# Attention output normalised in its transposed form, with row sums gathered by DMA

## The chip, the cores and the metric

The kernel runs on one core of a Trainium2 chip. Its time is the device time of one launch in microseconds (us), told as the median of three runs. One more launch was recorded by the hardware profiler; all rows below come from it.

## What is computed

One transformer block over x of 8 batches x 1024 tokens x 256: 16-head attention on the normalised input, and then a mixture-of-experts layer, each followed by a layer norm and a residual.

```
x = x + layernorm(attention(layernorm(x)))
x = x + layernorm(experts(layernorm(x)))

attention: q, k, v = split_heads(x @ w.T + b)         (16 heads of 16 columns)
           attn = softmax(q / sqrt(16) @ k.T)          (1024 x 1024 for each head)
           ctx  = attn @ v                             (joined to 256 columns)
           out  = ctx @ out_w.T + out_b
```

The change touches only the attention stage: how `ctx` is divided by the softmax's row sums and brought into the layout in which the output projection reads it.

## The kernel before

The program has two stages, one behind the other: attention (all 8 batches), then experts (16 groups of 512 tokens). Only the first is changed.

**Work of the attention stage.** A batch is cut into 8 steps of 8 units. Step s works on quad q = s // 2 (four heads) and on half f = s % 2 of the query tokens (512 of them); unit u = 8s + kc of the batch adds chunk kc of 128 keys. In a unit TensorE makes four score tiles (`st`, into `st_bank`), ScalarE takes their exponentials (`probs`), and TensorE multiplies them with the values (`pv`, into `o_bank`). For step s + 2 TensorE also makes four tiles of scores with the roles of queries and keys exchanged (`smax`, into three `sm_bank`s), and VectorE takes the maximum of each row (`reduce`, line 578). From these come the shifts of the exponentials: `combine_maxima` (line 585, two operands in SBUF), the job `SH` (a transposition), `shift_row`, and four small DMAs (`load_shift`) that put them into the stacked queries.

**Orders written by hand.** Each engine runs its own instruction list; semaphores join them. TensorE issues at most one job in a unit, by the table `JOBS`: (kind, batch offset, number, part). A job writes `job_bank`; ScalarE and VectorE read it one unit later. Jobs of half a projection are QK, V and OP (a unit each for its two parts), jobs of transpositions are XT, SH, OT and CT. `X_STATS`, `A_STATS` and `SEEDS` put VectorE's layer-norm work into units.

**The attention output before.** `o_bank` holds for each of the four heads 32 rows: 16 of output, one of the row sum (a column of ones behind the values, `VW = DH + 1`), the rest unused. At the first unit of the next step ScalarE copies it to `o_sb` (`store_o`, line 501). Job OT (8 per batch, units 10, 18, ... and unit 2 of the next batch) transposes it with four 128 x 128 passes, VectorE takes the reciprocals of the sums (line 623, 128 x 16) and multiplies (line 627) into `ctx_tok`, tokens on partitions. Job CT (4 per batch, units 0, 3, 11 and 12 of the next batch) transposes `ctx_tok` back, and ScalarE and VectorE split it in a high and a low part (`cT`, lines 478 and 605). Job OP (the output projection, units 5 to 8, 15, 16, 20, 21) reads `cT`.

**Pool** (GpSimd) normalises x for the next batch, adds the output bias (line 738), does the Newton steps of the reciprocal roots (lines 719 to 725), the normalisation of the attention output (751), the residual (755) and the copies of the values (744). **SP** issues every DMA, in one list: 14 for each quad's stack of queries and keys (`load_stack`, lines 220 and 224), 4 for each `load_shift` (line 233), and the loads and stores of x.

Units and steps are told here by their number in the batch; unit 64 is unit 0 of the next one. Waits on a counter stand in the instruction list, so what is queued behind a waiting instruction on its engine waits too.

## Time and profile before

| | us |
|---|---|
| median of three runs | 2961.0 (2960.58 to 2962.13) |
| profiled execution, its own time | 2961.11 |
| span of the profiled execution | 2959.3 |
| attention stage, up to its last store | 0 to about 1707 |
| one batch in the middle of it (492.72 to 689.99) | 197.27 |
| expert stage | from about 1710 |

Busy shares of the whole span are 95% for TensorE, 76% for VectorE, 56% for ScalarE and 18% for Pool; TensorE's granted clock is at its full level (2.4 GHz) in nearly all slices, and falls at the start and between the stages. These shares mix two stages with different limits, so the attention stage is read by batches and units. A timeline row gives start, duration, engine, line, operation and operands; rows of equal instructions that follow each other are merged, with their number behind x.

### The profile page before, as it was taken

The numbers are of one execution on the slowest core, as the hardware profiler recorded it, in microseconds if no ns is written. First come the engines' busy times: TensorE is split into PE (matmuls) and PEld (weight loads), VectorE is DVE, ScalarE is ACT, GpSimd is POOL, SyncE is SP. The second block draws the span as 40 slices with busy tenths as digits, with TensorE's granted clock in tenths as the row PEclk, the third lists the DMA queues.
The fourth block names the chain that finished last, engine by engine and source line by source line (L and its number), as shares of the span: only waits on it lengthen the run. The fifth ranks groups of instructions, "written<-read, shape, count | busy, mean of one in ns | idle before, by whom it ended". The sixth has DMA issues, their size and how long they took to land. (4 is left out here: it accounts for less than half of the span.)

```text
span 2959.3 us, 47558 instructions
## 1 busy us (share of the span) xinstructions
PE 2805.3 (95%) x16898; PEld 1718.8 (58%) x16898; DVE 2259.0 (76%) x4788; ACT 1643.3 (56%) x3095; POOL 541.0 (18%) x664
## 2 busy tenths in 40 slices
PE   5999999999999999999999659999999999999997
PEld 3434443443444434434443348888888888888886
DVE  5898999999989999999898146666666666666654
ACT  1577777777777777777777424333333333333332
POOL 4010220310312203103112220111111111111112
PEclk8899999999999999999999769999999999999999
DMA  5203332233133322330330033222322222232221
GB/s 91 44 17 50 44 73 38 51 51 52 31 58 45 73 37 51 52 51 17 57 44 23 22 110 108 79 79 79 78 78 79 80 79 79 78 78 79 79 72 54
DMA packets 120396, 180.59 MB, mean 61 GB/s; under 512 B 14160, under 2 KB 76768, under 8 KB 118112
## 3 DMA queue, kind: packets, MB, share of 16 engines
q1 hardware_dynamic: 120160, 177.55, 27.6%
q8 instruction: 135, 2.21, 0.3%
q14 instruction: 101, 0.83, 0.1%
HBM read 108.81 MB, written 17.30 MB: 43 GB/s over the span
## 5 line engine op out<-in xcount | busy, mean ns | idle before, releaser
L578 DVE TENSOR_REDUCE score_max<-sm_bank 128x1 f32<-128x512 f32 x2048 | 1305.2, 681 | 115.8 <-PE sm_bank L314 107.9
L511 ACT ACTIVATE probs<-st_bank 128x512 f32<-128x512 f32 x2048 | 1097.8, 598 | 346.8 <-PE st_bank L302 345.0
L314 PE MATMUL sm_bank<-qk_stack 64*128 64x512 f32 x2048 | 793.2, 462 | 21.6 <-DMA qk_stack<-qk_stack 10.6
L302 PE MATMUL st_bank<-qk_stack 64*128 64x512 f32 x2048 | 748.0, 449 | 21.7 <-ACT probs L511 20.8
L314 PEld LDWEIGHTS sm_bank<-qk_stack 64*128 64x128 f32 x2048 | 327.2, 187 | 574.8 <-DVE score_max L578 529.3
L324 PE MATMUL o_bank<-probs,v_quad 128*32 128x512 f32 x4096 | 545.4, 605 | 8.5 <-ACT o_sb L501 7.3
L1263 DVE TENSOR_TENSOR gated<-gate_act,u_bank 128x512 f32<-128x512 f32 x256 | 175.8, 687 | 311.1 <-ACT gate_act L1094 311.1
L1094 ACT ACTIVATE gate_act<-g_bank 128x512 f32<-128x512 f32 x272 | 162.5, 598 | 429.0 <-PE u_bank L1000 428.8
L302 PEld LDWEIGHTS st_bank<-qk_stack 64*128 64x128 f32 x2048 | 307.9, 184 | 72.3 <-ACT probs L511 49.3
L1105 ACT ACTIVATE h_hi<-h 128x512 fp32r<-128x512 f32 x272 | 172.0, 632 | 317.8 <-DVE h L1266 283.3
L1014 PE MATMUL y_bank<-f_w_hi,h_hi 128*128 128x256 f32 x1088 | 311.8, 287 | 5.9 <-DVE h_lo L1274 5.8
L1014 PE MATMUL y_bank<-f_w_hi,h_lo 128*128 128x256 f32 x1088 | 305.1, 280 | 0.0
L1014 PE MATMUL y_bank<-f_w_lo,h_hi 128*128 128x256 f32 x1088 | 303.7, 279 | 0.0
L1364 POOL TENSOR_SCALAR f_x_in<-f_x_in,f_mv,f_rstd 128x256 f32<-128x256 f32 x64 | 90.8, 1431 | 707.3 <-DVE f_rstd L1175 707.3
L1274 DVE TENSOR_TENSOR h_lo<-h,h_hi 128x512 fp32r<-128x512 f32 x272 | 185.5, 682 | 44.9 <-ACT h_hi L1105 41.6
L1000 PE MATMUL g_bank<-f_xT_lo,f_w_hi 128*128 128x512 f32 x544 | 216.7, 398 | 0.0
L1000 PE MATMUL g_bank<-f_xT_hi,f_w_hi 128*128 128x512 f32 x544 | 215.2, 396 | 1.5 <-DVE gated L1263 1.5
L1000 PE MATMUL g_bank<-f_xT_hi,f_w_lo 128*128 128x512 f32 x544 | 216.1, 397 | 0.0
L1000 PE MATMUL u_bank<-f_xT_hi,f_w_hi 128*128 128x512 f32 x544 | 215.8, 397 | 0.0
L1000 PE MATMUL u_bank<-f_xT_lo,f_w_hi 128*128 128x512 f32 x544 | 215.6, 396 | 0.0
L1000 PE MATMUL u_bank<-f_xT_hi,f_w_lo 128*128 128x512 f32 x544 | 215.4, 396 | 0.0
L1014 PEld LDWEIGHTS y_bank<-f_w_hi,h_hi 128*128 128x128 f32 x1088 | 205.3, 189 | 16.7 <-DVE h_lo L1274 6.5
(186 smaller groups left out, 3490.7 us busy)
## 6 DMA issues: line engine op xcount, KB each, us to landing
cb<-comb_dram SPq DMA_DIRECT2D x256, 256.0 KB, 3.7
qk_stack<-qk_parts SPq DMA_DIRECT2D x384, 128.0 KB
x_in<-in_x SPq DMA_DIRECT2D x8, 1024.0 KB, 6.4
x_res<-in_x SPq DMA_DIRECT2D x16, 512.0 KB, 3.8
x<-x_res SPq DMA_DIRECT2D x16, 512.0 KB, 2.9
f_x_in<-x SPq DMA_DIRECT2D x16, 512.0 KB, 3.9
f_x_res<-x SPq DMA_DIRECT2D x16, 512.0 KB, 7.1
out<-f_x_res SPq DMA_DIRECT2D x16, 512.0 KB, 3.2
```

Source lines behind the costliest of these rows:

```text
L302: mm(st_bank[tile % RING][:, :], k_stack[q][p][rows, kc * CH:(kc + 1) * CH], q_stack[q][p][rows, f * HALF:(f + 1) * HALF], start=True, sto ...
L314: mm(sm_bank[n % RING][:, :], q_stack[q][p][rows, tok:tok + CH], k_stack[q][p][rows, half * HALF:(half + 1) * HALF], start=True, stop=True ...
L324: last = mm(o_bank[32 * j:32 * j + 32, :], v_quad[q][:, kc, VW * j:VW * j + 32], probs[0 if kc % 2 == 0 else 1][:, j, :], start=(kc == 0), ...
L511: nc.scalar.activation(probs[kc % 2][:, j, :], st_bank[(4 * U + j) % RING][:, :], ACT.Exp).then_inc(exp_done, 1)
L578: v.reduce_max(score_max[f][:, HC * (2 * p + e) + c, half:half + 1], sm_bank[n % RING][:, :], AX_X).then_inc(smax_read, 1)
L1000: last = mm(bank[:, :], w[b][:, e, col + k * HID:col + (k + 1) * HID], xT[par][a][:, k, :], start=(t == 0), stop=(t == len(steps) - 1))
L1014: last = mm(y_bank[:, c, :], h[i][a][:, c * CH:(c + 1) * CH], w[b][:, e, 2 * D:3 * D], start=(e == 0 and t == 0 and c % 2 == 0), stop=(e = ...
L1094: a_(gate_act[i][:, :], g_bank[i][:, :], ACT.Silu).then_inc(S["silu_done"], 1)
L1105: a_(h[i][0][:, :], h32[i][:, :], ACT.Copy).then_inc(S["h_hi_done"], 1)
L1263: v.tensor_tensor(gated[:, :], gate_act[i][:, :], u_bank[i][:, :], ALU.mult).then_inc(S["gated_done"], 1)
L1274: v.tensor_tensor(h[i][1][:, :], h32[i][:, :], h[i][0][:, :].bitcast(F32), ALU.subtract).then_inc(S["h_ready"], 1)
L1364: gp.tensor_scalar(x_in[:, c, :], x_in[:, c, :], mv[:, c, 0:1], rstd[:, c:c + 1], ALU.subtract, ALU.mult).then_inc(S["f_x_normed"], 1)
```

## The change

- `VW` becomes 32: behind the 16 columns of values stand 16 columns of ones, so each head has 16 rows of output and 16 equal rows of sums in `o_bank`. The matmul's shape (128 x 32 weights) stays. The ones are set once, by Pool, in `v_quad`; the setting of `v_stage` by VectorE goes.
- The jobs OT and CT go, with VectorE's small reciprocals and multiplications, and `ctx_tok`. `store_o` stays.
- `gather` (SP, 8 DMAs of 32 KB per step, 64 per batch): the 16 output rows of each head go to `o_part[f]`, its sum rows to `sum_part[f]`, at the partitions in which the projection wants them. Two quads fill one such tile of 128 x 512.
- Four times a batch (f, k): VectorE writes a first guess of the reciprocal from the bits of the sums (`sum_recip`, one 128 x 512 operation, units 27, 35, 59 and 4 of the next batch), Pool does three Newton steps and the multiplication (`divide`, ten 128 x 512 tensor_tensor), and ScalarE and VectorE split the result (`split_hi`, `split_lo`, units 39, 46, 3, 11), now from SBUF. The very last one uses VectorE's reciprocal in place of guess and steps.
- `cT` becomes one pair for each half. `qk_parts` is halved in size, the first batch's second half of it lies in `probs`; the first exponential therefore waits for stacks 2 and 3 of batch 0, and stack 3 is loaded ahead of the first `load_shift(0, 1)`.

```diff
+SPLITS = {39: (0, 0, 0), 46: (0, 1, 0), 3: (-1, 0, 1), 11: (-1, 1, 1)}
+RECIPS = {27: (0, 0, 0), 35: (0, 1, 0), 59: (0, 0, 1), 4: (-1, 1, 1)}
 JOBS = {
-    0: ("CT", -1, 0, None), 3: ("CT", -1, 1, None), 11: ("CT", -1, 2, None), 12: ("CT", -1, 3, None),
-    2: ("OT", -1, 7, None),
...
-    if _s:
-        JOBS[8 * _s + 2] = ("OT", 0, _s - 1, None)
...
+            def gather(B, s):
+                q, f = s // 2, s % 2
+                if q % 2 == 0 and B + q > 0:
+                    sp.wait_ge(ctx_split, split_no(B, f, 0) + 1 if q else split_no(B - 1, f, 1) + 1)
+                sp.wait_ge(o_stored, STEPS * B + s + 1)
+                for j in range(4):
+                    to = 64 * (q % 2) + DH * j
+                    sp.dma_start(o_part[f][to:to + DH, :], o_sb[32 * j:32 * j + DH, :]).then_inc(gathered, 16)
+                    sp.dma_start(sum_part[f][to:to + DH, :], o_sb[32 * j + DH:32 * j + 2 * DH, :]).then_inc(gathered, 16)
...
             def batch(b, first, last, next_last):
                 if not first:
+                    gather(b - 1, 7)
                     load_residual(b - 1, 0)
                 load_shift(b, 1)
-                if first:
-                    sp.wait_ge(stacks_set, 5 * QUADS)
-                else:
+                if not first:
                     load_stack(b, 2, False)
-                load_stack(b, 3, first)
-                load_shift(b, 2)
-                load_shift(b, 3)
-                load_shift(b, 4)
+                    load_stack(b, 3, False)
+                for s in range(3):
+                    gather(b, s)
+                    load_shift(b, s + 2)
...
+                gather(b, 3)
                 load_shift(b, 5)
                 if not last:
                     load_stack(b + 1, 0, False)
+                gather(b, 4)
                 load_shift(b, 6)
                 if not first:
                     store_x1(b - 1, 1)
                 if not last:
                     load_stack(b + 1, 1, False)
+                gather(b, 5)
                 load_shift(b, 7)
+                gather(b, 6)
                 if not last:
                     load_shift(b, 8)
...
+            def split_hi(B, f, k):
+                act.wait_ge(divided, split_no(B, f, k) + 1)
...
+                nc.scalar.activation(cT[f][0][:, k, :], o_part[f][:, :], ACT.Identity,
+                                     bias=bias[:, 2, k:k + 1]).then_inc(ctx_hi, 1)
...
+                        if j == 0 and U == 0:
+                            act.wait_ge(stack_loaded[2], STACK_INC)
+                            act.wait_ge(stack_loaded[3], STACK_INC)
...
+            def sum_recip(B, f, k):
+                dve.wait_ge(gathered, GATHER_INC * (STEPS * B + 4 * k + 2 + f + 1))
+                n = split_no(B, f, k)
+                if n:
+                    dve.wait_ge(divided, n)
+                if n + 1 < split_no(BATCHES, 0, 0):
+                    v.tensor_scalar(recip[:, :].bitcast(I32), sum_part[f][:, :].bitcast(I32), -1, RECIP_SEED,
+                                    ALU.mult, ALU.add).then_inc(recip_begun, 1)
+                else:
+                    v.reciprocal(recip[:, :], sum_part[f][:, :]).then_inc(recip_begun, 1)
+            def split_lo(B, f, k):
+                dve.wait_ge(ctx_hi, split_no(B, f, k) + 1)
+                v.scalar_tensor_tensor(cT[f][1][:, k, :], o_part[f][:, :], bias[:, 2, k:k + 1],
+                                       cT[f][0][:, k, :].bitcast(F32), ALU.add, ALU.subtract).then_inc(ctx_split, 1)
...
+            def divide(B, f, k):
+                n = split_no(B, f, k)
+                wait_apart(pool, recip_begun, n + 1, passed["pool"])
+                if n + 1 < split_no(BATCHES, 0, 0):
+                    for i in range(3):
+                        if i:
+                            pool.wait_ge(recip_chain, 9 * n + 3 * i)
+                        g.tensor_tensor(recip_tmp[:, :], sum_part[f][:, :], recip[:, :], ALU.mult).then_inc(recip_chain, 1)
+                        pool.wait_ge(recip_chain, 9 * n + 3 * i + 1)
+                        g.tensor_tensor(recip_tmp[:, :], two[:, :].to_broadcast([128, HALF]), recip_tmp[:, :],
+                                        ALU.subtract).then_inc(recip_chain, 1)
+                        pool.wait_ge(recip_chain, 9 * n + 3 * i + 2)
+                        g.tensor_tensor(recip[:, :], recip[:, :], recip_tmp[:, :], ALU.mult).then_inc(recip_chain, 1)
+                    wait_apart(pool, recip_chain, 9 * (n + 1), passed["pool"])
+                g.tensor_tensor(o_part[f][:, :], o_part[f][:, :], recip[:, :], ALU.mult).then_inc(divided, 1)
...
             def batch(b, first, last):
                 copy_v(b, 3, first)
                 if not first:
+                    divide(b - 1, 1, 1)
                     add_bias(b - 1, 0)
                 if not last:
                     norm_x(b + 1)
                 if not first:
                     residual(b - 1, 0)
                     add_bias(b - 1, 1)
+                divide(b, 0, 0)
+                divide(b, 1, 0)
+                if not first:
                     residual(b - 1, 1)
                 if not last:
                     for q in range(3):
                         copy_v(b + 1, q, False)
+                divide(b, 0, 1)
```

Where the two lists of an engine stand apart, three places show it. VectorE, before, in units 1 to 4 of batch 1 (`cT_lo` is the second half of a CT job, `recip` and `ctx_tok` an OT job, the reductions are the row maxima):

```order
L605 SCALAR_TENSOR_TENSOR cT_lo<-job_bank,bias,cT_hi 128x512
L578 TENSOR_REDUCE score_max<-sm_bank 128x1 x4
L616 TENSOR_SCALAR shift_row<-job_bank 16x128
...
L623 RECIPROCAL recip<-job_bank 128x16
L627 TENSOR_TENSOR ctx_tok<-job_bank,recip 128x4x64
L578 TENSOR_REDUCE score_max<-sm_bank 128x1 x4
L605 SCALAR_TENSOR_TENSOR cT_lo<-job_bank,bias,cT_hi 128x512
```

VectorE, changed, units 3 to 4 and the first of unit 8 of a batch:

```order
L660 SCALAR_TENSOR_TENSOR cT_lo<-o_part,bias,cT_hi 128x512
...
L653 TENSOR_SCALAR recip<-sum_part 128x512
...
L618 TENSOR_TENSOR row_max<-score_max 128x16
L611 TENSOR_REDUCE score_max<-sm_bank 128x1 x2
L571 BN_STATS stats<-x_in 128x6
```

The reads of `job_bank` are gone; one operation on `o_part` and one on `sum_part` take their place, both with all operands in SBUF. SP, before, from the end of stack 3 (`load_stack(b, 3)`) on:

```order
L220 DMA qk_stack<-qk_parts 16x2048
L220 DMA qk_stack<-qk_parts 16x2x1024
L224 DMA qk_stack<-qk_stack 1x2x1024 x2
L233 DMA qk_stack<-shift_row 1x4x128 x12
L242 DMA x<-x_res 128x4x256
```

SP, changed, the same place:

```order
L248 DMA qk_stack<-qk_stack 1x2x1024 x2
L268 DMA o_part<-o_sb 16x512
L269 DMA sum_part<-o_sb 16x512
L268 DMA o_part<-o_sb 16x512
L269 DMA sum_part<-o_sb 16x512
L268 DMA o_part<-o_sb 16x512
L269 DMA sum_part<-o_sb 16x512
L268 DMA o_part<-o_sb 16x512
L269 DMA sum_part<-o_sb 16x512
L257 DMA qk_stack<-shift_row 1x4x128 x4
```

Eight DMAs of `gather` now stand between the stack and the shifts of step 2. Pool, changed, behind the bias of the second half: of what ran there before (the residual's Newton steps on 128 x 4) a `divide` of ten such rows now stands ahead, and another:

```order
L777 TENSOR_TENSOR attn_out<-attn_out,out_bias 128x512 x2
L786 TENSOR_TENSOR recip_tmp<-sum_part,recip 128x512
L788 TENSOR_TENSOR recip_tmp<-two,recip_tmp 128x512
L791 TENSOR_TENSOR recip<-recip,recip_tmp 128x512
...
L793 TENSOR_TENSOR o_part<-o_part,recip 128x512
```

## Rows read from the trace of the kernel before

**Rows 1.** Windows: length; busy PE, PEld, DVE, ACT, POOL; clock; DMA share; GB/s.

```profile
492.72:689.99 197.27, 193.87 (x1242) 79.94 (x1240) 184.32 (x346) 153.39 (x290) 38.77 (x62) 1.00 0.29 50
```

**Rows 2.** Timeline of TensorE, units 16 to 19 of that batch.

```profile
542.79 1.07 PE L324 MATMUL o_bank<-probs,v_quad 128*32 128x512 f32 x8
546.02 1.07 PE L324 MATMUL o_bank<-probs,v_quad 128*32 128x512 f32 x8
548.72 1.06 PE L324 MATMUL o_bank<-probs,v_quad 128*32 128x512 f32 x8
551.68 1.06 PE L324 MATMUL o_bank<-probs,v_quad 128*32 128x512 f32 x8
```

**Rows 3.** Timeline of VectorE, units 3 and 4 of that batch.

```profile
503.18 0.17 DVE L542 BATCH_NORM_AGGREGATE mv_x<-stats 128x2 f32<-128x6 f32 x1
503.27 0.22 DVE L623 RECIPROCAL recip<-job_bank 128x16 f32<-128x16 f32 x1
503.53 0.42 DVE L627 TENSOR_TENSOR ctx_tok<-job_bank,recip 128x256 f32<-128x256 f32 x1
503.87 2.47 DVE L578 TENSOR_REDUCE score_max<-sm_bank 128x1 f32<-128x512 f32 x4
506.26 0.74 DVE L605 SCALAR_TENSOR_TENSOR cT_lo<-job_bank,bias,cT_hi 128x512 fp32r<-128x512 f32 x1
506.92 0.68 DVE L578 TENSOR_REDUCE score_max<-sm_bank 128x1 f32<-128x512 f32 x1
```

**Rows 4.** Timeline of VectorE: statistics of x between two pairs of row maxima.

```profile
514.04 0.42 DVE L538 BATCH_NORM_STATS2 stats<-x_in 128x6 f32<-128x256 f32 x1
514.38 1.32 DVE L578 TENSOR_REDUCE score_max<-sm_bank 128x1 f32<-128x512 f32 x2
```

**Rows 5.** Durations by line (minimum/median/maximum in ns): a VectorE operation on 128 x 512 in SBUF.

```profile
L638 DVE TENSOR_SCALAR x_res<-probs x1: 427/427/427, 11.0 to 11.0; 128x512 f32<-128x512 f32 x1
```

**Rows 6.** Groups of instructions of the batch: Pool on 128 x 512 in SBUF.

```profile
L738 POOL TENSOR_TENSOR attn_out<-attn_out,out_bias 128x512 f32<-128x512 f32 x4 | 5.1, 1278 | 28.4 <-ACT attn_out L484 28.4
```

**Rows 7.** Timeline of the stage's end: ScalarE, Pool and SP.

```profile
1661.67 0.60 ACT L501 ACTIVATE o_sb<-o_bank 128x512 f32<-128x512 f32 x1 [1.18 <-PE o_bank L324]
1680.37 0.20 POOL L719 TENSOR_TENSOR newton_a<-rstd_a 128x4 f32<-128x4 f32 x1 [2.02 <-DVE rstd_a L560]
1680.64 0.20 POOL L721 TENSOR_TENSOR newton_a<-newton_a,var_a 128x4 f32<-128x4 f32 x1
1691.19 2.48 POOL L738 TENSOR_TENSOR attn_out<-attn_out,out_bias 128x512 f32<-128x512 f32 x2
1706.63 0.37 SPq L242 DMA_DIRECT2D x<-x_res  x1
```

**Rows 8.** Timeline of SP's DMA issues, units 2 to 27 of the batch.

```profile
500.45 2.43 SPq L233 DMA_DIRECT2D qk_stack<-shift_row  x4
...
516.29 11.10 SPq L220 DMA_DIRECT2D qk_stack<-qk_parts  x12
527.44 1.32 SPq L224 DMA_DIRECT2D qk_stack<-qk_stack  x2
528.80 47.54 SPq L233 DMA_DIRECT2D qk_stack<-shift_row  x12
```

**Rows 9.** Timeline of ScalarE and SP ahead of the first unit.

```profile
77.65 35.67 SPq L233 DMA_DIRECT2D qk_stack<-shift_row  x8
102.32 3.10 ACT L511 ACTIVATE probs<-st_bank 128x512 f32<-128x512 f32 x6
```

**Rows 10.** Timeline, VectorE beside Pool: once in the expert stage, once in attention.

```profile
2913.76 2.40 POOL L1375 TENSOR_TENSOR f_x_res<-y,f_x_res 128x1024 f32<-128x1024 f32 x1 [0.18 <-POOL y L1371]
2914.60 2.10 DVE L1266 TENSOR_TENSOR h<-gated,cb 128x512 f32<-128x512 f32 x1
...
564.41 4.83 POOL L751 TENSOR_SCALAR attn_out<-attn_out,mv_a,rstd_a 128x256 f32<-128x256 f32 x4 [0.22 <-POOL rstd_a L725]
...
567.47 0.17 DVE L585 TENSOR_TENSOR row_max<-score_max 128x16 f32<-128x16 f32 x1
```

More of the change, by code:

```diff
@@ L17 @@
 RING = 3
-VW = DH + 1
+VW = 2 * DH
 EXPERTS, HID, TOPK = 16, 128, 8
@@ L441, in _ @@
                 batch(b, b == 0, b == BATCHES - 1)
-            job("OT", BATCHES - 1, 7)
-            for i in range(2):
-                job("CT", BATCHES - 1, i)
-            for i in range(2):
-                job("OP", BATCHES - 1, i)
-            for i in range(2, 4):
-                job("CT", BATCHES - 1, i)
-            for i in range(2, 4):
+            for i in range(4):
                 job("OP", BATCHES - 1, i)
@@ L516, in batch @@
                         kind, off, i, part = JOBS[u - 1]
-                        if kind in ("XT", "QK", "V", "CT", "OP") and part != 0:
+                        if kind in ("XT", "QK", "V", "OP") and part != 0:
                             job(kind, b + off, i)
+                    if u in SPLITS and not (first and SPLITS[u][0]):
+                        off, f, k = SPLITS[u]
+                        split_hi(b + off, f, k)
             for b in range(BATCHES):
@@ L522, in _ @@
             store_o(STEPS * BATCHES)
-            for f in range(2):
-                for kind in ("CT", "OP"):
-                    for i in (2 * f, 2 * f + 1):
-                        job(kind, BATCHES - 1, i)
+            split_hi(BATCHES - 1, 0, 1)
+            job("OP", BATCHES - 1, 0)
+            job("OP", BATCHES - 1, 1)
+            split_hi(BATCHES - 1, 1, 1)
+            job("OP", BATCHES - 1, 2)
+            job("OP", BATCHES - 1, 3)
         @block.vector
@@ L673, in batch @@
                         reduce(S + 2, (s + 2) % STEPS, kc, 0)
+                    if u in SPLITS and not (first and SPLITS[u][0]):
+                        off, f, k = SPLITS[u]
+                        split_lo(b + off, f, k)
+                    if u in RECIPS and not (first and RECIPS[u][0]):
+                        off, f, k = RECIPS[u]
+                        sum_recip(b + off, f, k)
                     if not last and u in X_STATS:
@@ L692, in _ @@
                 batch(b, b == 0, b == BATCHES - 1)
-            job("OT", BATCHES - 1, 7)
+            split_lo(BATCHES - 1, 0, 1)
+            sum_recip(BATCHES - 1, 1, 1)
             for f in range(2):
-                job("CT", BATCHES - 1, 2 * f)
-                job("CT", BATCHES - 1, 2 * f + 1)
+                if f == 1:
+                    split_lo(BATCHES - 1, 1, 1)
                 for c in range(HC):
@@ L757, in _ @@
             pool.sem_inc(x1_ready, 1)
+            g.memset(two[:, :], 2.0).then_inc(two_set, 1)
+            wait_apart(pool, two_set, 1, passed["pool"])
             set_stacks(0)
```

116 lines of the change are left out of this document (54 added, 62 removed).

## The prediction

> **What bounds the kernel now.** I read the table of windows first: in one batch of 197.27 us TensorE is busy for 193.87 and VectorE for 184.32, ScalarE has a fifth to spare and Pool is idle for 158 [rows 1]. Two engines are almost full, so the next view is the timeline of TensorE, unit by unit, from one group of `pv` matmuls to the next. Unit 16 carries half a projection and takes 546.02 - 542.79 = 3.23; unit 17 carries only SH, 2.70; unit 18 carries OT, 2.96 [rows 2]. All 64 spacings of the batch, read in this way, fall into these kinds: 32 units with half a projection at 3.19 to 3.23, where TensorE sets the pace; light ones at 2.70 to 2.75; single transposition jobs at 2.90 to 2.96; and some at 3.04 to 3.49, which are in units 1 to 4 and 11 to 13.
>
> Those last ones are VectorE's. Four row maxima back to back take 506.26 - 503.87 = 2.39, and up to 2.47 with the start of the next; I use 2.47 a unit. An OT job costs it 503.87 - 503.27 = 0.60, a CT job 506.92 - 506.26 = 0.66 [rows 3]. Statistics of x cost 514.38 - 514.04 = 0.34 [rows 4], their aggregation 503.27 - 503.18 = 0.09 [rows 3], so 0.44 together. So units with a CT or OT read and statistics come to 3.0 to 3.13, above a light unit's 2.70, and the three score banks let VectorE lag by about a microsecond before TensorE waits. In units with half a projection VectorE has 0.75 to spare.
>
> **What goes.** Batches 1 to 6, by groups of units, spacing now against the larger of 2.70 (2.91 with XT) and VectorE's new sum:
> - Units 0 to 4 take 15.30 now. New: 5 x 2.47, two statistics 0.88, SH and `row_max` 0.30, one split 0.66, one guess 0.4: 14.6. Saved 0.7.
> - Units 9 to 14 take 17.98. New: 6 x 2.47, three statistics 1.32, SH 0.2, one split 0.66: 17.0. Saved 1.0.
> - Units 18 and 19 take 6.05, new 5.4. Saved 0.6.
> - Units 26 and 27: 0.2; 33 and 34: 0.35; 42, 50 and 58, each 2.91 to 2.70: 0.6.
> The sum is 3.45, say 3.4 a batch. In units with half a projection nothing is saved, and the 48 transposition passes are worth less than their TensorE time, since part of it filled waits.
>
> The guess (`sum_recip`) is not in the trace in its form. A tensor_scalar on 128 x 512 in SBUF took 0.43 [rows 5], the split on as many elements 0.74 [rows 3]; I take 0.4 of pitch, near the first, because it is the same kind of operation. At the upper end the four cost 0.3 more each, of which units 27, 35 and 59 hide theirs and unit 4 doesn't: 0.3 a batch.
>
> **What comes, beside other work.** A `divide` is ten tensor_tensor on 128 x 512 in a chain. Pool does one in 1.28 [rows 6]; from one Newton step to the next the pitch is 0.27 for an operation of 0.20 [rows 7], a gap of 0.07. So 10 x 1.28 + 9 x 0.07 = 13.4, with the start about 13.7, 4.4 units. Pool's 39 us a batch become 39 + 4 x 13.4 = 92 of 194. Each result is due later: the guess of unit 27 ends in unit 32 and is split in 39; 35 in 40, for 46; 59 in 0, for 3; 4 in 9, for 11. The tightest, the last, has nearly two units left, and the bias and residual work behind it waits for no more than it did. Pool's length is hidden.
>
> The gathers are 8 issues a step. Four small issues take 2.43, 0.6 each; a stack's larger ones 11.10 / 12 = 0.93 [rows 8]. I take 0.6, the row with the small transfer, so 4.8 a step; SP's list has the room. The place to look at is behind stacks 2 and 3. Now their last issue ends at about 528.8 and the shifts of step 2 go straight behind [rows 8]. With `gather(b, 0)` ahead they are issued by 528.8 + 4.8 + 2.4 = 536.0. TensorE wants them for the first score tile of step 2, about 0.66 ahead of the `pv` of unit 15, which started 3.23 before 542.79 [rows 2]: at 538.9, and some 1.0 sooner in the changed kernel, 537.9. That leaves 1.9 for landing: taken as nothing, 1.9 a batch if the gathers issue at 0.93. The shifts of step 6 stand the same way behind `gather(b, 4)`, with half a microsecond less at stake.
>
> Batch 0: the first exponential waits for stack 3. The shift ahead of it starts at 77.65, takes 2.4, then 14 issues of 0.93 end at 93.1; the first exponential is at 102.32 [rows 9]. Hidden by 9 us. Were that cover gone it would cost up to the 13 us of the stack.
>
> **What comes, in the way.** VectorE's `row_max` and `split_lo` read two tensors in SBUF, and so does Pool's tensor_tensor. In the expert stage one such VectorE operation was started 0.84 into a Pool tensor_tensor and took 2.10 in place of 0.69, ending 0.54 behind Pool's end: it stood still for 1.41. Beside a Pool tensor_scalar `row_max` took its usual 0.17 [rows 10]. Now Pool hardly does a tensor_tensor in attention while VectorE reads two SBUF tensors. In the changed kernel `row_max` of unit 8 and `split_lo` of unit 39 fall inside a `divide`; `row_max` of units 32, 40 and 64 fall at or just behind the end of one. A stop lasts as long as what is left of one Pool operation, 0 to 1.28, 0.64 on average. At unit 64 VectorE sets the pace: I charge 0.4 (it may miss). At unit 8 a fifth is absorbed: 0.5. At 32 the slack of half-projection units takes it: 0. At 39 two splits, the QK one and the new one, meet a stop, 2.47 + 1.32 + 0.64 = 4.4 against 3.22, and unit 40 adds `row_max`: a lag of 1.5 of which a microsecond is bearable; 0.6. Together 1.5 a batch (0 to 6.4, all five whole and none absorbed).
>
> The Trainium skill, "SBUF — State Buffer", section "Who interferes with whom", says that a VectorE instruction with two SBUF inputs and a GpSimd instruction that reads SBUF lock each other out for the whole instruction, the later one waiting. The first pair of rows agrees, with 1.41; the second does not, since `row_max` ran through beside a tensor_scalar.
>
> **The stage's end.** From the last `store_o` at 1661.67 to the last store at 1706.63 it is 45.0 [rows 7]. Now half 0 goes first, on the chain OT, CT, CT, OP, OP, bias, statistics, and Pool's Newton steps start at 1680.37; half 1's bias waits for Pool until 1691.19. New: the divide of (7, 0, 1) begins in unit 60, about 1651, and ends at 1664.6; split 1.5, two OP jobs of 3.5 each: 1673.2. The gather of step 7 lands at about 1661.7 + 0.7 + 4.8 + 2 = 1669.2; the reciprocal takes 0.43 at least [rows 5], and I take 0.7, then Pool's multiplication, 1671.2; bias, statistics and seed of half 0 end at about 1676.8, which is 3.5 before 1680.37, and what follows on Pool keeps its length. 3 saved. The reciprocal's far end is 7.0 (0.22 for 16 columns [rows 3], scaled by 32), which would turn this into a loss of 3.
>
> **The sum.** Batches 1 to 6: 6 x (3.4 - 1.5) = 11.4. Batch 0 has no OT 7 and no CT: by its own spacings 2.0, less 0.5. Batch 7 has no row maxima in its last steps, where an OT unit is as long as a light one (2.68): 2.9, less 0.5. End 3. Together 18.3: the profiled execution goes from 2961.11 to 2943, and so does the median, which lies 0.1 from it. The expert stage is unchanged.
>
> **The rivals.**
> - *Pool's stops don't reach TensorE.* For: a stop is short, `row_max` is tiny. Against: units 0 to 4 leave no slack. 6 x 3.4 + 4.9 + 3 = 28: 2933. Chance 0.25.
> - *The shifts come late.* `gather` moves the shifts of steps 2 and 6 behind 16 more issues. For: 1.9 us of room. Against: the 0.6 of the small issues. 1.9 + 0.8 a batch, seven batches, 19: 2962, within 0.2% of before. Chance 0.12.
> - *Slower: the shared access to SBUF.* One mechanism, at units 8, 32, 39, 40 and 64 while Pool divides: all stops near 1.28, and not absorbed, since behind units 8, 32 and 40 VectorE-bound units follow. Six batches x (6.4 - 3.4) = 18, batches 0 and 7 about even, end -3: 2976 at most, 2968 in the middle. It decides from 3.4 a batch, which is 0.68 a stop with nothing absorbed. By the rule of the Trainium skill's page named above this is the case, since each of the five is a lock-out. Chance 0.18.
> - The forecast itself, 2943: 0.45.
>
> **How the numbers follow.** A difference within 0.2% (5.9 us) can't be told from none. The forecast and the first rival are faster: 0.70. The late shifts are mostly the same: 0.13 with a rest of the others. Slower: 0.17. The range goes down to 2931, below the first rival by the error of its sum, and up to 2964, over the late shifts and to the nearer part of the slower case; beyond it I leave somewhat under 0.2.
>
> **What would show it.** Units 18, 42, 50 and 58 at 2.70; batches of 195.4 in place of 197.27 (193.9 without stops, 200 with whole ones); durations of `row_max` above 0.17 and of `split_lo` above 0.74 in units 8 and 39; no wait of `st` for a DMA of the shifts; Pool near 92 us a batch; the last store 42 behind the last `store_o`. The prediction is wrong if `sum_recip` waits for a gather (VectorE idle before it), if Pool's operations on 128 x 512 are longer than 1.28 so that a split waits, or if the DMA issues are.

## The result, and the profile after

The changed kernel takes 2942.4 us (median of four runs, 2941.2 to 2944.3) against 2961.1 for the kernel before, run beside it on the same chip: a ratio of 0.9937, with an interval of 0.9920 to 0.9954. The profiled execution spans 2942.6 us where that of before spans 2959.3, so 16.7 less; it was the slowest of the four (2944.3). The last store of the attention stage is issued at 1690.62, before at 1706.63 [rows 7].

First the page of the changed kernel: busy time of each engine, and its DMA issues with size and time to landing. Pool went from 18% to 31%.

```profile
PE 2772.4 (94%) x16514; PEld 1689.3 (57%) x16514; DVE 2241.8 (76%) x4691; ACT 1635.6 (56%) x3095; POOL 916.9 (31%) x976
...
o_part<-o_sb SPq DMA_DIRECT2D x256, 32.0 KB, 1.9
sum_part<-o_sb SPq DMA_DIRECT2D x256, 32.0 KB, 2.0
```

The same batch as in [rows 1], in windows (length; busy PE, PEld, DVE, ACT, POOL; clock; DMA share; GB/s), of the changed kernel:

```profile
488.96:683.43 194.47, 189.98 (x1194) 76.61 (x1192) 181.90 (x334) 152.36 (x290) 86.87 (x103) 1.00 0.34 61
```

TensorE has 3.9 us less to do and the batch is 2.8 shorter, with 48 matmuls fewer; Pool has 48 us more, and no engine waits for a result of Pool's. The units of [rows 2], 16 to 19, in the changed kernel:

```profile
537.35 1.06 PE L364 MATMUL o_bank<-probs,v_quad 128*32 128x512 f32 x8
540.57 1.06 PE L364 MATMUL o_bank<-probs,v_quad 128*32 128x512 f32 x8
543.27 1.07 PE L364 MATMUL o_bank<-probs,v_quad 128*32 128x512 f32 x8
546.24 1.06 PE L364 MATMUL o_bank<-probs,v_quad 128*32 128x512 f32 x8
548.95 1.06 PE L364 MATMUL o_bank<-probs,v_quad 128*32 128x512 f32 x8
```

Read as there: unit 16 3.22, unit 17 2.70, unit 18 2.97, unit 19 2.71. Unit 18 kept its 2.97 though its transposition job is gone, and unit 19 fell to a light unit from 3.09 (6.05 for the two before, less the 2.96 of [rows 2]). In unit 18 TensorE waits for VectorE to read a score bank, here as a timeline row of TensorE in that unit:

```profile
545.21 0.50 PE L354 MATMUL sm_bank<-qk_stack 64*128 64x512 f32 x1 [0.21 <-DVE score_max L611]
```

VectorE has statistics of the attention output and the shifts to make there besides its row maxima, so it is VectorE that holds this unit at 2.97.

Between batches there is now a spread that the kernel before did not have. From step 0 to step 0, batches 1 to 6 take 194.90, 194.47, 197.76, 194.18, 195.36 and 194.19; before, each took 197.2 to 197.3. The reason stands in the table of waits of the changed kernel, window 300 to 1500 (engine, tile and line, what was waited for: us in total, times, longest):

```profile
PEld st_bank L342 <- DMA qk_stack<-shift_row: 7.0, 6, 2.6
PE st_bank L342 <- DMA qk_stack<-shift_row: 4.6, 4, 2.2
```

TensorE waits for the shifts. The longest of these is in the batch of 197.76. Timeline of SP and TensorE there, around units 13 to 15 (start, duration, engine, line, operation, operands, number; in brackets the wait ahead of it and its releaser):

```profile
717.20 1.85 SPq L248 DMA_DIRECT2D qk_stack<-qk_stack  x2
719.15 0.58 SPq L268 DMA_DIRECT2D o_part<-o_sb  x1
...
721.04 1.62 SPq L269 DMA_DIRECT2D sum_part<-o_sb  x1
...
724.85 0.58 SPq L269 DMA_DIRECT2D sum_part<-o_sb  x1
725.48 2.53 SPq L257 DMA_DIRECT2D qk_stack<-shift_row  x4
...
729.69 0.57 PE L342 MATMUL st_bank<-qk_stack 64*128 64x512 f32 x2 [2.19 <-DMA qk_stack<-shift_row]
...
730.35 1.85 PE L364 MATMUL o_bank<-probs,v_quad 128*32 128x512 f32 x8
```

The eight issues of `gather` stand between the stack and the shifts, one of them at 1.62 in place of 0.59. The shifts are issued by 728.01 and TensorE goes on at 729.69. Its `pv` group behind the wait then takes 1.85 in place of 1.06, and the windows say why (same columns as above):

```profile
724.00:728.00 4.00, 3.25 (x21) 1.22 (x21) 3.58 (x7) 2.95 (x6) 0.00 (x0) 1.00 0.14 34
728.00:732.00 4.00, 2.31 (x11) 0.45 (x11) 2.07 (x5) 1.28 (x3) 0.00 (x0) 0.81 0.01 3
732.00:736.00 4.00, 4.00 (x26) 2.01 (x22) 2.62 (x7) 2.54 (x5) 0.00 (x0) 0.76 0.02 5
736.00:740.00 4.00, 4.00 (x30) 1.82 (x26) 3.52 (x9) 2.87 (x7) 1.41 (x7) 1.00 0.21 52
```

The granted clock falls from 1.00 to 0.81 and 0.76, so part of these windows ran at the lower of its two levels (1.2 in place of 2.4 GHz): (0.19 + 0.24) x 4.00 = 1.7 us of full clock are missing, which is 3.4 us at half. It is back from 736 on. Units 14 and 15 took 4.80 and 4.78 where 2.74 and 3.24 are usual.

The second thing to look at are VectorE's two-operand reads beside Pool. Timeline of both at unit 8, and at unit 39, of the batch from 488.96:

```profile
513.82 1.28 POOL L791 TENSOR_TENSOR recip<-recip,recip_tmp 128x512 f32<-128x512 f32 x1
513.91 1.23 DVE L618 TENSOR_TENSOR row_max<-score_max 128x16 f32<-128x16 f32 x1
...
608.76 1.28 POOL L793 TENSOR_TENSOR o_part<-o_part,recip 128x512 f32<-128x512 f32 x1 [0.18 <-POOL recip L791]
609.65 0.94 DVE L660 SCALAR_TENSOR_TENSOR cT_lo<-o_part,bias,cT_hi 128x512 fp32r<-128x512 f32 x1
```

`row_max`, 0.17 alone, is started 0.09 into Pool's operation and ends 0.04 behind it. `split_lo`, 0.74 alone, takes 0.94. The durations of `row_max` between 300 and 1500 (minimum/median/maximum in ns) show that most of the 49 miss Pool; the long ones are those of unit 8, one in each batch:

```profile
L618 DVE TENSOR_TENSOR row_max<-score_max x49: 174/176/1253, 319.0 to 1489.7; 128x16 f32<-128x16 f32 x49
```

Third, the end of the stage, to be read against [rows 7]. Timeline of the last `pv`, the last `store_o`, the last reciprocal, Pool and SP:

```profile
1645.44 1.94 PE L364 MATMUL o_bank<-probs,v_quad 128*32 128x512 f32 x8 [1.16 <-ACT probs L539]
1647.44 0.60 ACT L519 ACTIVATE o_sb<-o_bank 128x512 f32<-128x512 f32 x1 [2.05 <-PE o_bank L364]
1654.63 3.35 DVE L656 RECIPROCAL recip<-sum_part 128x512 f32<-128x512 f32 x1 [5.20 <-DMA sum_part<-o_sb]
1658.16 1.26 POOL L793 TENSOR_TENSOR o_part<-o_part,recip 128x512 f32<-128x512 f32 x1 [11.07 <-DVE recip L656]
1659.38 2.48 POOL L777 TENSOR_TENSOR attn_out<-attn_out,out_bias 128x512 f32<-128x512 f32 x2
...
1690.62 0.37 SPq L277 DMA_DIRECT2D x<-x_res  x1
```

From the last `store_o` to the last store it is 43.18, before 44.96. The bias of half 0 stands behind Pool's multiplication, and that waits for a reciprocal of 3.35.

### The profile page after: what moved, and what is told of

It reads as the page before. It is cut to its first block and busy times, and to the rows that moved or that the text cites. A ratio compares the mean times of both kernels' runs of the same rounds, so it can differ in the third digit from the quotient of the medians.

```text
span 2942.6 us, 47567 instructions
## 1 busy us (share of the span) xinstructions
PE 2772.4 (94%) x16514; PEld 1689.3 (57%) x16514; DVE 2241.8 (76%) x4691; ACT 1635.6 (56%) x3095; POOL 916.9 (31%) x976
## 5 line engine op out<-in xcount | busy, mean ns | idle before, releaser
L354 PE MATMUL sm_bank<-qk_stack 64*128 64x512 f32 x2048 | 804.1, 465 | 18.6 <-DMA qk_stack<-qk_stack 10.9
L342 PE MATMUL st_bank<-qk_stack 64*128 64x512 f32 x2048 | 761.6, 453 | 37.9 <-ACT probs L539 31.3
L342 PEld LDWEIGHTS st_bank<-qk_stack 64*128 64x128 f32 x2048 | 316.7, 184 | 119.3 <-ACT probs L539 91.7
L786 POOL TENSOR_TENSOR recip_tmp<-sum_part,recip 128x512 f32<-128x512 f32 x93 | 119.2, 1282 | 488.4 <-DVE recip L653 483.5
```

What stands on the lines that cost most here:

```text
L342: mm(st_bank[tile % RING][:, :], k_stack[q][p][rows, kc * CH:(kc + 1) * CH], q_stack[q][p][rows, f * HALF:(f + 1) * HALF], start=True, sto ...
L354: mm(sm_bank[n % RING][:, :], q_stack[q][p][rows, tok:tok + CH], k_stack[q][p][rows, half * HALF:(half + 1) * HALF], start=True, stop=True ...
L786: g.tensor_tensor(recip_tmp[:, :], sum_part[f][:, :], recip[:, :], ALU.mult).then_inc(recip_chain, 1)
```

## The experiments

Each is measured beside the kernel before, on the same chip, but the groups ran on different chips, on which the kernel before took 2959.4 to 2961.1. So differences of about 1 us between groups mean little. The attention stage's end (issue of the last store of x) is given beside the time, because the expert stage, the same in all kernels, took 1251.5 to 1254.8 in the profiled executions compared here, a spread that small differences drown in.

**The two suspects of the prediction, one at a time.** The first kernel takes the `gather`s out of the shifts' way at four places:

```diff
                 for s in range(3):
-                    gather(b, s)
                     load_shift(b, s + 2)
+                    gather(b, s)
...
-                gather(b, 4)
                 load_shift(b, 6)
+                gather(b, 4)
```

> The changed kernel with load_shift ahead of gather for steps 2, 3, 4 and 6; nothing else moves. Theory (gathers push the shifts of step 2 past the moment at which TensorE wants them, and TensorE's clock falls in the gap): the waits of st for the shift DMAs, 11.6 us between 300 and 1500 in the changed kernel's trace, vanish, batches all take 194.2, unit 14 is 2.7 in each; 5 to 8 us less than the changed kernel, 2935 to 2938. Rival (TensorE's waits there only stand in for VectorE's, which would end as late): within 1.5 us of the changed kernel.

Measured: 2994.1 us, ratio 1.0117 (1.0103 to 1.0130); the stage ends at 1738.27. No theory had this. Unit 14 is at 2.73 in every batch, so the late shifts are gone; but a new wait has come, in each batch at the guess of unit 27. Timeline of SP and VectorE of this kernel:

```profile
781.41 2.51 SPq L257 DMA_DIRECT2D qk_stack<-shift_row  x4
783.96 0.56 SPq L268 DMA_DIRECT2D o_part<-o_sb  x1
...
788.35 0.59 SPq L269 DMA_DIRECT2D sum_part<-o_sb  x1
...
790.32 0.43 DVE L653 TENSOR_SCALAR recip<-sum_part 128x512 int32<-128x512 int32 x1 [4.91 <-DMA sum_part<-o_sb]
```

`gather(b, 2)` now stands behind `load_shift(b, 4)`, whose own data, the shifts of step 4, are made only in units 24 to 26. So the rows of step 2, ready since unit 24, leave SP at 783.96 to 788.94, and VectorE stands before `sum_recip` for 4.91 with all its row maxima queued behind it. TensorE's row behind it, and the windows from there on (columns as before):

```profile
791.40 0.79 PE L354 MATMUL sm_bank<-qk_stack 64*128 64x512 f32 x1 [4.24 <-DVE score_max L611]
...
790.90:797.72 6.82, 6.32 (x24) 2.49 (x24) 5.43 (x10) 2.95 (x6) 6.41 (x6) 0.50 0.58 167
```

TensorE stands still for 4.24, and then its granted clock is at the lower level for 6.8. Units 28 and 29 take 8.82 and 4.50 in place of 3.12 and 3.22: 7.0 more, of which 4.2 are the wait and the rest falls in the stretch at the lower level. The same edit with the next one added (below) gave 2993.3, ratio 1.0112: the same wait, where the two gains had been expected to add.

The expectation above counts TensorE's waits for the shifts as 11.6. That adds PEld's 7.0 and PE's 4.6, which are the same landings seen twice; by the lengths of units 14 and 15 it is 5.7 in batches 1 to 6.

> The shifts ahead of the gathers, and the one-input row_max together. Theory: the two gains add, 7 to 11 us less than the changed kernel, 2932 to 2936, and 25 to 29 less than the kernel before. Rival (they hide behind the same units): no more than the larger of the two alone.

**Take away what meets Pool.** `row_max` as a reduction, which has one operand in SBUF:

```diff
-                v.tensor_tensor(row_max[:, :], score_max[f][:, :, 0], score_max[f][:, :, 1],
-                                ALU.max).then_inc(row_max_ready, 1)
+                v.reduce_max(row_max[:, :], score_max[f][:, :, :], AX_X).then_inc(row_max_ready, 1)
```

> The changed kernel with row_max made by one tensor_reduce over the two halves' columns in place of a tensor_tensor, so that it reads one SBUF tensor. Theory (a VectorE operation with two SBUF inputs stops behind a Pool tensor_tensor): row_max never takes above 0.3, unit 8 goes from 3.50 to 3.22, 2 to 3.5 us less than the changed kernel. Rival (the stop is of the access to SBUF as such, or the long row_max is absorbed): unit 8 stays at 3.50, within 0.8 us of the changed kernel.

Measured: 2943.0 (2938.9 to 2949.5), ratio 0.9945 (0.9933 to 0.9958). Timeline beside Pool at unit 8 of this kernel:

```profile
511.32 1.29 POOL L790 TENSOR_TENSOR recip<-recip,recip_tmp 128x512 f32<-128x512 f32 x1
511.39 0.19 DVE L618 TENSOR_REDUCE row_max<-score_max 128x16 f32<-128x32 f32 x1
```

Its durations between 300 and 1500 (minimum/median/maximum in ns):

```profile
L618 DVE TENSOR_REDUCE row_max<-score_max x49: 185/186/188, 317.5 to 1483.3; 128x16 f32<-128x32 f32 x49
```

The reduction runs through inside Pool's operation, in all 49 cases. Unit 8 goes from 3.50 to 3.22 and unit 9 from 2.78 to 2.71 in batches 1 to 6. The mechanism is shown, and its price with it: 0.35 a batch. The time as a whole didn't fall by the 2 to 3.5 that were expected. In its profiled execution the late shifts take 4.1 in units 14 and 15 (one unit 14 of 4.33), against 2.1 in the second profile of the changed kernel (below), which is most of what the reduction gains; and its times spread over 10 us.

The next kernel leaves out Pool's three Newton steps (the output is divided with the rough guess), so that Pool hardly works:

```diff
-                if n + 1 < split_no(BATCHES, 0, 0):
+                if False:
                     for i in range(3):
```

> The changed kernel with the nine Newton operations of each divide left out (the first guess is multiplied as it is, so the division is rough); Pool does one 128x512 tensor_tensor in place of ten. Theory (Pool's 13 us a divide are hidden, and cost only the stops of row_max and split_lo): like the kernel with the one-input row_max and 0.2 a batch more, 3 to 5 us less than the changed kernel. Rival (Pool's length matters, since later work on Pool ends later): 8 us or more less.

Measured: 2942.1 (2939.6 to 2945.4), ratio 0.9940 (0.9927 to 0.9952). Units 8 and 9 are at 3.22 and 2.71 again, unit 40 at 3.21 in place of 3.26; unit 39 stays at 3.33, so that is not Pool's doing: two splits fall in it on ScalarE too. 36 of Pool's operations a batch removed give 0.35 in units 8 and 9 and 0.05 in unit 40, and nothing in the other units of batches 1 to 6, those of the late shifts aside. Pool's length is hidden. The time missed its 3 to 5 as well: its late shifts take 7.5 in its profiled execution.

**The late shifts, without the new wait.** Only the two `gather`s whose place matters are moved; `gather(b, 2)` stays ahead of `load_shift(b, 4)`. The changed kernel was run again beside it:

```diff
-                for s in range(3):
+                load_shift(b, 2)
+                gather(b, 0)
+                for s in range(1, 3):
                     gather(b, s)
                     load_shift(b, s + 2)
...
-                gather(b, 4)
                 load_shift(b, 6)
+                gather(b, 4)
```

> The changed kernel as it is, for the comparison on one chip. Both theories expect 15 to 20 us less than the kernel before. Theory (the shift DMAs of step 2 land late by another amount in each execution): its unit 14s differ from batch to batch, 2.7 to 5, and its times spread by 3 to 8 us, where the kernel before spreads by 2 to 4.

> The changed kernel with only the shifts of steps 2 and 6 issued ahead of the gathers of steps 0 and 4, whose results VectorE wants much later; the other gathers stay where they are. Theory (late shifts cost the changed kernel 4 to 8 us, and the 50 us of the first reordering came from a late gather that VectorE waited for): 4 to 8 us less than the changed kernel, no wait for shift DMAs, unit 14 at 2.7 in all batches, no wait of the guess in units 27. Rival (any gather behind a shift delays something of its own): no less, or more than the changed kernel.

Measured: the changed kernel again 2943.0 (2942.3 to 2948.1); with the two moved 2937.5 (2936.6 to 2940.3), ratio 0.9926 (0.9914 to 0.9939), the stage's end at 1684.16. Timeline of SP in this kernel at the place shown above (its step began 1.0 sooner):

```profile
715.76 2.31 SPq L248 DMA_DIRECT2D qk_stack<-qk_stack  x2
718.11 2.49 SPq L257 DMA_DIRECT2D qk_stack<-shift_row  x4
720.70 0.58 SPq L268 DMA_DIRECT2D o_part<-o_sb  x1
```

The shifts leave SP straight behind the stack and no wait for them is left in the table of waits. So the late shifts cost 5.5 us of the changed kernel's time by the medians. By single executions it varies, as the wait does: the stage ends 6.5 sooner than in the first profile of the changed kernel, 2.6 sooner than in the second (1686.77), and units 14 and 15 hold 5.9 of it in the first and 2.1 in the second, whose unit 14s lie between 2.73 and 3.88.

**Both mended.** The two moved `gather`s and the reduction together:

> Those two shifts first and row_max with one SBUF input. Theory: unit 8 at 3.22 instead of 3.50 in seven batches and the last batch's unit 40 at 2.7 instead of 3.3: 2.5 us less than with the shifts alone, 22 to 28 less than the kernel before, with a spread below 3 us. Rival (the stops are absorbed): the same as with the shifts alone.

Measured: 2936.0 (2934.7 to 2936.5), ratio 0.9918 (0.9905 to 0.9932), the stage's end at 1680.39. In time 1.5 less than with the `gather`s alone, in the stage's end 3.8 less, of which 0.9 was there when step 1 of batch 0 began; unit 32 of batch 7 went from 3.26 to 2.71 and unit 8 of every batch but the first to 3.22. The expectation had named unit 40 of batch 7 for this; that stays at 3.66, since `split_lo` still meets Pool there. Its batch, in windows:

```profile
487.11:681.01 193.90, 189.45 (x1194) 76.35 (x1192) 181.03 (x334) 152.23 (x290) 86.84 (x103) 1.00 0.35 61
```

All six middle batches lie between 193.7 and 193.9.

**Where the 3.4 a batch are.** On this base, what the change took away is given back, to each engine apart and to both, without its waits for other engines: four 128 x 128 transpositions per step that nobody reads; and on VectorE one reduction over 128 x 512 per step (0.66, where an OT job cost 0.60).

```diff
+    JOBS[8 * _s + 2] = ("TR", 0, _s, None)
...
+                if kind == "TR":
+                    for c in range(HC):
+                        nc.tensor.transpose(job_bank[:, c * CH:(c + 1) * CH], ident[:, :], ident[:, :])
```

```diff
+                    if kc == 3:
+                        v.reduce_max(spare[:, S:S + 1], two_wide[:, :], AX_X)
```

> The kernel with the two shifts first and the one-input row_max, and with four 128x128 transpositions of a constant put back on TensorE in units 2, 10, ..., 58 of each batch (the places of the OT jobs; nobody reads them). Theory (a single transposition job costs a light unit 0.2): units 18, 26, 34, 42, 50 and 58 from 2.70 to 2.91, units 2 and 10 less since VectorE sets their pace: 8 to 12 us more than without them. Rival (the gain came from VectorE alone): under 3 us more.

> The same base with one VectorE operation of about 0.6 (a tensor_reduce on 128x512 in SBUF, no wait, nobody reads it) put back in units 3, 11, ..., 59, the places of the OT reads. Theory (VectorE has no slack in units 0 to 4 and 9 to 14 only): units 3, 11 and 19 longer, 1.2 to 2 us a batch, 8 to 15 us more in all. Rival (TensorE's jobs alone set the time): under 3 us more.

> Both put back. Theory (in a unit the longer of TensorE's and VectorE's work counts, and the lag of a microsecond joins neighbouring units): more than either, less than the sum, 15 to 22 us more than the base, which leaves only the CT jobs and the end of the stage as gain over the kernel before. Rival (they are independent): the exact sum.

Measured: TensorE's share back 2946.1, ratio 0.9947 (0.9934 to 0.9959); VectorE's 2951.3, 0.9965 (0.9951 to 0.9979); both 2957.2, 0.9988 (0.9980 to 0.9997). So 10.2, 15.3 and 21.2 more than the base, where the parts add up to 25.5; each is 0.7 less if measured from the kernel before, which took 0.7 more on this chip. The same batch in the three, in this order, one line of each kernel's windows:

```profile
489.75:684.84 195.09, 191.90 (x1226) 78.70 (x1224) 181.40 (x334) 152.88 (x290) 86.88 (x103) 1.00 0.34 61
```

```profile
491.36:687.26 195.90, 190.17 (x1194) 76.56 (x1192) 185.40 (x342) 152.54 (x290) 87.04 (x102) 1.00 0.34 61
```

```profile
492.50:689.20 196.70, 192.69 (x1226) 78.91 (x1224) 185.59 (x342) 153.12 (x290) 87.06 (x103) 1.00 0.34 61
```

TensorE is given 2.5 us more work and the batch grows by 1.2; VectorE 4.4 and it grows by 2.0. Unit by unit: the transpositions cost 0.21 each in units 2, 26, 34, 42, 50 and 58, of which unit 3 gives 0.08 back, and nothing in 10 and 18, which stay at 2.97 with or without them (the expectation had 18 growing). VectorE's reduction costs 0.60 in units 3 and 11 (2.78 to 3.38) and 0.28 in 19; the one of unit 27 costs 0.07 there and 0.2 in 28; those of 35, 43, 51 and 59 cost nothing in their own units.

Unit 40 grows too, by 0.28, and that is not VectorE's load. The reduction of unit 35 stands ahead of the guess, so Pool divides later and `split_lo` of unit 39 meets Pool's last multiplication at another point. Timeline of Pool and VectorE in the kernel with VectorE's share back:

```profile
612.55 1.29 POOL L798 TENSOR_TENSOR o_part<-o_part,recip 128x512 f32<-128x512 f32 x1 [0.18 <-POOL recip L796]
613.14 1.24 DVE L663 SCALAR_TENSOR_TENSOR cT_lo<-o_part,bias,cT_hi 128x512 fp32r<-128x512 f32 x1
```

It takes 1.24 here in every batch, 0.94 in the base and with TensorE's share back, and 1.09 with both. It was TensorE and VectorE both, in different units: 1.2 a batch for TensorE, 1.7 for VectorE, 0.3 for Pool's stop, which the test itself brought in.

**The stage's end.** Two kernels on the base of the two mended places. In one, the very last division uses the guess without Newton steps in place of VectorE's reciprocal, so that its result is rough:

```diff
-                if n + 1 < split_no(BATCHES, 0, 0):
+                if True:
                     v.tensor_scalar(recip[:, :].bitcast(I32), ...
```

> The same again, with VectorE's last reciprocal on 128x512 (3.35 us in the changed kernel's trace) replaced by the tensor_scalar guess (0.42), without Newton steps, so the last division is rough. Theory (this reciprocal lies on the chain that ends the stage): 2.9 us less than without this edit, and from the last store_o to the last store 40.3 instead of 43.2. Rival (half 0's own chain ends the stage, the reciprocal is beside it): under 0.8 us less.

Measured: 2932.3 (2930.9 to 2932.9), ratio 0.9906 (0.9892 to 0.9919), 3.7 under the base. Last `store_o` to last store 40.45 in place of 43.37: the 2.9 by which the operation is shorter, to the tenth. In the other, which computes all, the four DMAs of the sums go ahead of the four of the rows in the very last `gather`, with a semaphore of their own, and the reciprocal waits for them alone:

```diff
+                if isinstance(B, int) and B == BATCHES - 1 and s == STEPS - 1:
+                    for j in range(4):
...
+                        sp.dma_start(sum_part[f][to:to + DH, :],
+                                     o_sb[32 * j + DH:32 * j + 2 * DH, :]).then_inc(last_sums, 16)
+                    for j in range(4):
...
+                        sp.dma_start(o_part[f][to:to + DH, :], o_sb[32 * j:32 * j + DH, :]).then_inc(gathered, 16)
+                    return
...
+                    dve.wait_ge(gathered, GATHER_INC * (STEPS * BATCHES - 1))
+                    dve.wait_ge(last_sums, 64)
```

> The kernel with the two shifts first and the one-input row_max, and in the very last gather the four DMAs of sums issued ahead of the four of outputs, so that VectorE's last reciprocal starts while the outputs are still on their way (Pool's multiplication waits for them). Nothing is left out. Theory (the reciprocal of 3.35 us is on the chain that ends the stage, and the last four issues of 0.63 lie ahead of it): 2 to 2.5 us less than without this edit, 2933 to 2934. Rival (the outputs' landing or half 0's chain sets the end): under 0.8 us less.

Measured: 2933.8 (2932.0 to 2934.7), ratio 0.9906 (0.9889 to 0.9922), from last `store_o` to last store 40.64, which is 2.7 less than in the base. Timeline of SP and VectorE there:

```profile
1638.48 2.40 SPq L270 DMA_DIRECT2D sum_part<-o_sb  x4
1640.92 2.73 SPq L274 DMA_DIRECT2D o_part<-o_sb  x4
...
1642.33 3.35 DVE L671 RECIPROCAL recip<-sum_part 128x512 f32<-128x512 f32 x1 [2.48 <-DMA sum_part<-o_sb]
```

The reciprocal starts 4.5 behind `store_o` (1637.85) in place of 7.2. This is the best version that computes everything: 27 us under the kernel before, and some 9 under the changed one.

## Why the prediction was right, and where it was right by luck

It said 2943.0 and 2942.4 was measured. The total is right; of its terms the main one is, and two errors of about the same size cancel: that is luck. Terms and measured values, in the profiled executions (the changed kernel's was the slowest of four, and its late shifts the larger of the two that are known):

| term | predicted | measured |
|---|---|---|
| gain without stops, batches 1 to 6 | 6 x 3.4 = 20.4 | 6 x 3.4 = 20.4 |
| stops behind Pool, batches 1 to 6 | -9.0 | -2.0 |
| late shifts, batches 1 to 6 | 0 | -5.7 |
| batches 1 to 6 together | 11.4 | 12.7 |
| batch 0 | 1.5 | 1.4 |
| batch 7 up to the last `store_o` | 2.4 | 0.1 |
| stage's end | 3.0 | 1.8 |
| expert stage | 0 | 0.7 |
| sum | 18.3 | 16.7 |

**The gain per batch** held: 197.27 less 3.4 is 193.9, and the kernel without late shifts and without stops at `row_max` has a batch of 193.90. By groups: units 0 to 4 come to 14.0 (2.70, 2.79, 2.70, 2.79, 3.05 in that kernel) where the sum of VectorE's work gave 14.6, so that group gained 1.3 and not 0.7; units 42, 50 and 58 stand at 2.70 as worked out. Unit 18 did not come to 2.70 but stayed at 2.97, and so did 10: the prediction read the 2.96 before as the price of its transpositions, and it was VectorE's pace, so units 18 and 19 gained 0.4 and not 0.6. Units 33 and 34 gained 0.2 and not 0.35, and unit 28, behind the guess of 27, grew from 2.93 to 3.12, units 39 and 40 by 0.13 together, none of which was counted. So the 3.4 is itself a sum in which misses cancel. The 2.47 a unit for four row maxima is an upper figure; that VectorE's debt in a unit of 2.70 is paid out of the three banks fits this and isn't shown apart. Giving the work back bears out the reading behind it: TensorE's 2.5 us of passes are worth 1.2, and in most half-projection units VectorE's work costs nothing.

**The guess** took 0.41 to 0.43 as assumed. **Pool**: its operations took 1.28, the three of a `divide` with a broadcast operand 1.04, gaps 0.08 to 0.18; a `divide` lasts 12.9 and Pool is busy for 86.87 a batch, against 13.4 and 92. Hidden, as said. `sum_recip`, whose waiting for a gather was named as a sign of being wrong, waits for none between 300 and 1500. **Prologue**: hidden, as said; step 1 of batch 0 begins at 126.41, before 126.17.

**The stops** are the term that was mis-sized in one direction: 1.5 a batch against 0.33 (a batch of 194.18 without late shifts, less the 193.85 with the reduction). The mechanism of [rows 10] is right in both halves, and the experiment with the reduction shows it at unit 8. What failed is the step that counted meetings. Of five places, two meet Pool (8 and 39), and since Pool's chain starts at the same point of each batch, they do so in each batch alike, the others in none: there was nothing to average. At unit 39 ScalarE, with two splits, holds TensorE anyway. The page "SBUF — State Buffer" of the Trainium skill, section "Who interferes with whom", is borne out for two reading operands (0.17 became 1.23) and for the reduction, which it says does not contend (185 to 188 ns in all 49). That the VectorE operation stands until Pool's ends shows in `split_lo`: it lasted 0.94, 1.09, 1.24 and 1.58 in four places, and each time it ended 0.54 to 0.55 behind the end of the Pool operation it met. The slower rival rested on its rule for all five places, and here it needed the places to meet first.

Batch 7 shows what the same stops cost where they do meet, and its account closes. `row_max` of unit 32 (1.29 long) costs 0.57 there, and `split_lo` costs 0.84 in unit 40: without Newton steps that unit is 2.82, with them 3.66. Timeline of the changed kernel:

```profile
1559.06 1.28 POOL L793 TENSOR_TENSOR o_part<-o_part,recip 128x512 f32<-128x512 f32 x1 [0.18 <-POOL recip L791]
1559.09 1.29 DVE L618 TENSOR_TENSOR row_max<-score_max 128x16 f32<-128x16 f32 x1
...
1580.67 1.58 DVE L660 SCALAR_TENSOR_TENSOR cT_lo<-o_part,bias,cT_hi 128x512 fp32r<-128x512 f32 x1
```

With 0.28 at unit 8, 0.22 for a late shift and 0.87 for a last `pv` at the lower clock, the prediction's gain of 2.9 without stops becomes 2.9 - 2.8 = 0.1, the measured one. That last item is the clock's fall at the end of the stage, which comes just ahead of the group here. The window that holds it:

```profile
1645.30:1647.40 2.10, 1.94 (x8) 0.20 (x8) 0.00 (x0) 0.09 (x1) 1.62 (x2) 0.50 0.00 0
```

The group took 1.94 in five of the kernels and executions profiled (here, in the second run of this kernel, with the reduction alone, with both shares given back and in the best version) and 1.06 in the kernel before and eight others, in which the clock falls behind it. The gap ahead of the group is the same, 1.16 to 1.17; why the fall comes now ahead of it and now behind isn't shown.

**The late shifts** are the other. Their rival was priced at 19 us with a chance of 0.12 and the forecast charged nothing, and it named "no wait of `st` for a DMA of the shifts" as a sign; they cost 5.5 by the medians. Step by step, in the batch from 488.96: the forecast had the shifts issued 43.3 after the batch's start, and it is 532.37 - 488.96 = 43.4. The issues took 0.59 with a pitch of 0.63, as assumed. Demand is what failed: it was put at 45.2, and TensorE stood ready at 44.1, because up to unit 14 the kernel had gained 2.1 and not the 1.0 that the forecast had credited (by its own groups, 0.7 and 1.0 less 0.9 for stops). With a landing of 1.1 behind the last issue there is no room left, and TensorE waits 0.4. In the batches that wait longest, 1, 3 and 5 (0.84, 2.19 and 1.22), an issue of the stack or of `gather` took 1.2 to 1.6 in place of 0.6; in batch 3, through the clock, the wait became 3.6 for two units. "Taken as nothing" was wrong because 1.9 of room was compared with a landing that had no price. The Trainium skill, "DMA: Bandwidth & Descriptors", section "Anatomy of one DMA", gives about 2.0 us for the fixed part of a DMA that GpSimd issues. The `gather`s are issued by SP, for which this section has no figure; the page of the profile shows 1.9 and 2.0 from issue to landing for them.

The two errors are tied: fewer stops make the batch faster, and a faster batch asks for the shifts sooner. That the removal of the stops alone brought nothing measurable, and 1.5 us once the shifts were early, fits this. It isn't shown, since these waits vary by themselves: 4.6 and 1.3 us between 300 and 1500 in two executions of the same kernel.

**The stage's end**: the reciprocal was taken as 0.7 and measured 3.35, inside the bounds of 0.43 to 7.0 that the prediction named. It starts 7.2 behind the last `store_o`, forecast 7.5. So Pool's multiplication ends 12.0 behind, forecast 9.5, while the OP jobs of half 0 are read by 9.3, forecast 11.5. So the multiplication, and not the OP jobs, sets the bias, and 1.8 is saved and not 3.0. With the guess in its place, 2.9 come back.

Range and chances: 2942.4 lies in 2931 to 2964, faster. Among the cases, what happened is the first rival's mechanism (the stops barely reach TensorE) together with the second rival's, at a tenth to a third of its price (2.1 and 5.9 of 19 in the two profiles).

## What to carry to other kernels

Where one queue issues for several consumers, each DMA put into it has two neighbours: what stands behind it comes later by its issue time, and it comes later itself by the wait of what stands ahead. Price both, and compare the room with issue plus landing; moving four `gather`s for the first reason alone cost 51 us for the second, part of it through the clock. Before averaging a contention over chance, look whether the two sides have a fixed phase: work that starts from the same event in each batch meets always or never, and an edit elsewhere can move the phase. And a chance to be late grows with every microsecond that the rest of the change gains.

## What the runs showed of the hardware that was not expected

- VectorE's RECIPROCAL on 128 x 512 takes 3.35 us, eight times a tensor_scalar on as many elements (0.41 to 0.43), and far less than 32 times the 0.22 of 16 columns [rows 3].
- A wait of 2.2 us of TensorE was followed by 3.4 us at the lower level of the clock, and cost another 1.6 us. In the kernel with four `gather`s moved, a wait of 4.24 was followed by 6.8 us at that level. The wait of 1.2 us in another batch (unit 14 at 3.84) was followed by none: unit 15 took 3.23; nor was one of 1.7 with the reduction alone (unit 14 at 4.33, unit 15 at 3.23).
- Issues of small DMAs on SP mostly take 0.58 to 0.59, but of the 756 of `gather` and shifts in the changed kernel's trace from 105 to 1640, 25 took 0.8 to 1.9. Since the shifts had no room, times of the kernels with late shifts spread over 3 to 11 us, against 2 to 4 once the shifts had room.
- Pool's tensor_tensor with a broadcast first operand took 1.04 in place of 1.28.
